# Local attention with the scores transposed at birth: keys on partitions, a fixed shift in the exponent, row sums from columns of ones

## The reference, cut to what matters

```python
WIN = 16
idx = jnp.arange(s)[:, None] + jnp.arange(-WIN, 1)[None, :]
valid = idx >= 0
k_win = k_full[:, jnp.maximum(idx, 0)]
scores = jnp.einsum('bsh,bswh->bsw', x, k_win) * h ** (-0.5)
scores = jnp.where(valid[None], scores, -jnp.inf)
attn_out = jnp.einsum('bsw,bswh->bsh', jax.nn.softmax(scores, axis=-1), k_win)
x1 = _layernorm(x + attn_out, g1, be1)
...
gate = jax.nn.sigmoid(jnp.concatenate([x1, mo], axis=-1) @ Wg.T + bg)
combined = gate * x1 + (1.0 - gate) * mo
x2 = _layernorm(x1 + combined, g2, be2)
ff = jax.nn.silu(x2 @ W1.T + b1) @ W2.T + b2
```

## Time and profile before

| what | value |
|---|---|
| median of 3 runs | 2090.1 us (2085.8, 2090.1, 2090.33) |
| the profiled execution: its own time | 2084.03 us |
| its span, first to last instruction | 2082.0 us |
| mean granted TensorE clock | 0.942 |
| PE busy | 1885.0 us (91%) |
| DVE busy | 1579.9 us (76%) |
| ACT busy | 1091.3 us (52%) |
| POOL busy | 651.0 us (31%) |

### The profile page before, as it was taken

How to read it: one execution, slowest core, us unless ns; L and a number is a source line. 1 busy time by engine, 2 the same in 40 slices (tenths; PEclk the granted TensorE clock), 3 DMA queues, 4 the chain that set the end, 5 groups by cost and what they waited for, 6 DMA issues and landing times.

```text
span 2082.0 us, 32807 instructions
## 1 busy us (share of the span) xinstructions
PE 1885.0 (91%) x11942; PEld 1683.8 (81%) x11942; DVE 1579.9 (76%) x4165; ACT 1091.3 (52%) x1890; POOL 651.0 (31%) x872
## 2 busy tenths in 40 slices
PE   5888978999999999999579995889999769999996
PEld 4677867998989998898469984779989659999995
DVE  5665637999999999999758874678988736666663
ACT  4554544556656666655456643444544235555552
POOL 3333200123333343334513322123444412322332
PEclk9999989999999999999789997989999679999998
DMA  5545331012212112110234413213322212332210
GB/s 173 175 159 189 135 108 61 21 52 70 84 60 76 55 57 86 55 64 24 88 100 133 134 56 112 72 61 103 95 64 62 75 59 65 100 100 74 67 55 19
DMA packets 132344, 176.86 MB, mean 85 GB/s; under 512 B 11470, under 2 KB 115541, under 8 KB 132056
## 3 DMA queue, kind: packets, MB, share of 16 engines
q1 hardware_dynamic: 121432, 159.74, 24.0%
q0 software_dynamic: 10752, 15.04, 2.2%
HBM read 113.19 MB, written 76.41 MB: 91 GB/s over the span
## 4 chain that ended last, share of the span: by engine, by line
PE 71%; DVE 17%; DMA 4%; issue 4%; ACT 2%; POOL 1%; SPq 1%; POOLq 0%; DVEq 0%; ACTq 0%
PE ps L362 63%; PE ps L386 5%; DVE bst L1346 3%; DMA xa<-in_x 2%; PE ps L657 2%; DVE xl L1360 1%; DVE xl L1365 1%; DVE fl L1534 1%; DVE kl L1371 1%; DVE f1l L1418 1%; DVE xl L1568 1%; POOL d_p L2131 1%; SPq L2259 1%; DVE pay L1654 1%; DVE hl L1434 0%
## 5 line engine op out<-in xcount | busy, mean ns | idle before, releaser
L362 PE MATMUL ps<-wslotA,fh 128*128 128x256 f32 x1792 | 327.5, 283 | 0.0
L362 PEld LDWEIGHTS ps<-wslotA,fh 128*128 128x128 f32 x1792 | 284.1, 191 | 6.8 <-DVE fl L1534 0.2
L1534 DVE TENSOR_TENSOR fl<-fF,fh 128x512 fp32r<-128x512 f32 x320 | 214.7, 684 | 92.7 <-ACT fF L1016 92.7
L2126 POOL TENSOR_TENSOR smalls<-smalls,powers 128x4 f32<-128x4 f32 x104 | 41.2, 396 | 714.0 <-DVE smalls L1349 713.9
L362 PE MATMUL ps<-wslotA,fl 128*128 128x256 f32 x896 | 253.4, 283 | 0.0
L362 PE MATMUL ps<-x2h,wslotA 128*128 128x512 f32 x512 | 181.4, 406 | 0.0
L362 PEld LDWEIGHTS ps<-wslotA,fl 128*128 128x128 f32 x896 | 171.3, 191 | 0.0
L1015 ACT ACTIVATE fh<-ps,b1e 128x512 fp32r<-128x512 f32 x128 | 88.3, 690 | 148.5 <-PE ps L362 146.3
L2131 POOL DMA_INDIRECT d_p<-pay,sut x128 | 137.5, 1074 | 65.1 <-issue 38.5
L362 PE MATMUL ps<-wslotB,fh 128*128 128x256 f32 x768 | 139.8, 283 | 0.0
L362 PE MATMUL ps<-eh,wslotB 128*128 128x512 f32 x384 | 126.6, 396 | 4.1 <-DVE el L1732 4.1
(11 more groups left out here) (349 smaller groups left out, 5424.4 us busy)
## 6 DMA issues: line engine op xcount, KB each, us to landing
stage<-in_w SPq DMA_DIRECT2D x16, 1024.0 KB, 5.7
d_p<-pay SPq DMA_DIRECT2D x24, 528.0 KB, 5.3
pay<-d_p SPq DMA_DIRECT2D x24, 528.0 KB, 3.8
xa<-in_x SPq DMA_DIRECT2D x16, 512.0 KB, 6.3
d_h<-hh SPq DMA_DIRECT2D x16, 512.0 KB, 4.6
d_h<-hl SPq DMA_DIRECT2D x16, 512.0 KB, 2.7
xl<-in_x SPq DMA_DIRECT2D x16, 512.0 KB, 3.9
hh<-d_h SPq DMA_DIRECT2D x16, 512.0 KB, 5.3
```

What stands on the lines that cost most here:

```text
L362: return pe.matmul(o, a, b, start=start, stop=stop, skip_group_check=True)
L1534: ve.tensor_tensor(fl[n % 2][:, half(k)], fF[n % 2][:, half(k)], f32(fh[n % 2][:, half(k)]), ALU.subtract).then_inc(S["low"], 1)
L2126: last(po.tensor_tensor(t[:, 8:12], mv_of(t)[:, :, 1], eps, ALU.add))
```

## The change

Scores are computed with keys on partitions: for each tile of 128 keys the 128 queries of the same tile and the first 16 of the next one (144 columns). What comes out of the exponent is already the stationary operand of `attend`, so `p_t`, `p_turned` and `pT` go, and with them one unit of the ring. The shift of the exponent is the constant -16, so the maximum, its bias and the four separate activations become one activation over 576 columns. Each tile of `xl` gets two more columns that hold ones (258 a tile, 4128 bytes a group), and `attend` gives the row sums in column 256. 258 columns don't fit twice into a bank, so `attend` now takes two units, AV0 and AV1, one after the other. `halo` copies one tile and only in even groups. `sc` is double. `Wg1T` and `Wg2T` are loaded into `pay[0]`, which makes them wait for the zero fills that read it, and the load of `xl3` waits for nothing of `qc`.

```diff
 def scores(g):
     evacuated("XT", g)
     ps = unit("SC", g)
...
+    for i in range(4):
+        n = 144 if i < 3 else 128
         for c in range(2):
             o = c * 512 + i * 128
-            t = mm(ps[:, i * 256:i * 256 + 160], q[:, o:o + 128], q[:, o - 32:o + 128], c == 0 and i == 2, c == 1)
+            mm(ps[:, i * 256:i * 256 + n], q[:, o:o + 128], q[:, o:o + n], c == 0 and i % 2 == 0, c == 1)
+    for c in range(2):
+        t = mm(ps[:, 896:912], before[:, c * 512 + 384:c * 512 + 512], q[:, c * 512:c * 512 + 16], False, c == 1)
     t.then_inc(S["sc"], 1)
...
-def p_t(g):
-    pe.wait_ge(S["ex"], g + 1)
-    ps = unit("PT", g)
...
 def attend(g):
-    evacuated("PT", g)
-    pe.wait_ge(S["halo"], g + 1)
-    ps = unit("AV", g)
+    pe.wait_ge(S["ex"], g + 1)
+    pe.wait_ge(S["halo"], g // 2 + 1)
+    x, p = xl[g % 4], sc[g % 2]
+    units = [unit("AV", g, k) for k in range(2)]
     for i in range(4):
+        mm(units[i // 2][:, half(i % 2, 258)], p[:, i * 144:i * 144 + 128], x[:, i * 258:i * 258 + 258],
+           True, i == 0 and g % 2 == 0)
     for i in range(0 if g % 2 else 1, 4):
+        o = (i - 1) % 4 * 144 + 128
+        rows_ = x[:, (i - 1) * 258:i * 258] if i else halo_t
+        t = mm(units[i // 2][0:16, half(i % 2, 258)], p[:, o:o + 16], rows_, False, True)
+        if i % 2:
+            t.then_inc(S["av"], 1)
...
 def exponent(g):
-    act.wait_ge(S["mx"], g + 1)
-    s = sat_at(g)
-    for i in range(4):
-        q = sc[:, i * 160:(i + 1) * 160]
-        t = act.activation(q, q, ACT.Exp, bias=s[:, 4 + i:5 + i], scale=1.0 / 16.0, accum_out=s[:, 8 + i:9 + i])
+    u, q = ring.of("SC", g), sc[g % 2][:, 0:576]
+    act.wait_ge(u.free, u.before + 1)
+    act.activation(q, q, ACT.Exp, bias=bound, scale=1.0 / 16.0).then_inc(S["ex"], 1)
...
 def memory(n):
     if n == 0:
+        ve.wait_ge(S["mpe"], 2)
+        ve.wait_ge(S["prep_dve"], 1)
+        for i in range(4):
+            ve.memset(v3(xl[i], 4, 258)[:, :, 256:258], 1.0)
...
 def halo(g):
+    if g % 2 == 0:
+        ve.wait_ge(S["xn"], g + 1)
+        if g:
+            ve.wait_ge(S["av"], 2 * g)
+        ve.tensor_copy(halo_t, xl[g % 4][:, 774:1032]).then_inc(S["halo"], 1)
...
 def masked(g):
-    last(ve.tensor_reduce(s[:, 0:4], scv, AX.X, ALU.max))
-    ve.tensor_scalar(s[:, 4:8], s[:, 0:4], -1.0 / 16.0, None, ALU.mult).then_inc(S["mx"], 1)
+    ve.tensor_tensor(v3(sc[g % 2][:, 0:576], 4, 144), v3(u.ap, 4, 256)[:, :, 0:144],
+                     bandm.unsqueeze(1).to_broadcast([128, 4, 144]), ALU.add).then_inc(u.free, 1)
...
 def attended(g):
-    u, s, x = ring.of("AV", g), sat_at(g), xv(xl[g % 4])
+    s, x = sat_at(g), xw(xl[g % 4])
+    ve.wait_ge(S["av"], 2 * g + 2)
+    for k in range(2):
+        u = ring.of("AV", g, k)
+        pv = v3(u.ap, 2, 512)
+        last(ve.reciprocal(s[:, 12 + 2 * k:14 + 2 * k], pv[:, :, 256]))
+        for i in (2 * k, 2 * k + 1):
+            t = ve.scalar_tensor_tensor(x[:, i, :], pv[:, i % 2, 0:256], s[:, 12 + i:13 + i], x[:, i, :],
+                                        ALU.mult, ALU.add)
+        t.then_inc(u.free, 1)
...
     square(mw_v, "mem_W", S["qabc"])
+if s == 12:
+    sp.wait_ge(S["fill"], 384)
     square(wg2_v, "Wg2T", S["qabc"])
     square(wg1_v, "Wg1T", S["qabc"])
```

More of the change, by code:

```diff
@@ L32 @@
 TILES_AT = SMALL_AT + 20608
[L33 removed]
+CONST_AT = TILES_AT + 19 * PAGE + 128
 class Count:
@@ L381, in mm256, with turn @@
                 return t
-            def turn(ps, x, signal):
+            def turn(ps, x, signal, stride=256):
                 for c in range(2):
@@ L581, in x_t @@
                 pe.wait_ge(S["xn"], g + 1)
-                turn(unit("XT", g), xl[g % 4], S["xnT"])
+                turn(unit("XT", g), xl[g % 4], S["xnT"], 258)
             def scores(g):
@@ L586, in scores @@
                 ps = unit("SC", g)
[L587 to L593, removed]
+                q, before = xT[g % 2], xT[(g - 1) % 2 if g % 2 else 0]
@@ L643, in x2_t @@
                 pe.wait_ge(S["x2"], g + 1)
-                turn(unit("X2T", g), xl[g % 4], S["x2T"])
+                turn(unit("X2T", g), xl[g % 4], S["x2T"], 258)
             def t_t(which, g, x):
@@ L1515, in clear_pay @@
             def clear_pay():
-                for i in (1, 2):
+                for i in range(3):
                     ve.memset(pay_v[i][:, :, 261:264], 0.0)
@@ L1557, in masked @@
-                s = sat_at(g)
-                ve.wait_ge(u.free, u.before + 1)
-                last(ve.tensor_reduce(s[:, 0:4], scv, AX.X, ALU.max))
-                ve.tensor_scalar(s[:, 4:8], s[:, 0:4], -1.0 / 16.0, None, ALU.mult).then_inc(S["mx"], 1)
-            def attended(g):
-                u, s, x = ring.of("AV", g), sat_at(g), xv(xl[g % 4])
-                ve.wait_ge(S["ex"], g + 1)
-                last(ve.reciprocal(s[:, 12:16], s[:, 8:12]))
-                ve.wait_ge(S["av"], g + 1)
-                for i in range(4):
-                    t = ve.scalar_tensor_tensor(x[:, i, :], u.ap[:, i * 256:(i + 1) * 256], s[:, 12 + i:13 + i], x[:, i, :],
-                                                ALU.mult, ALU.add)
-                t.then_inc(u.free, 1)
+                if g >= 2:
+                    ve.wait_ge(S["av"], 2 * (g - 1))
@@ L1572, in stats_1st @@
             def stats_1st(g):
-                u = ring.of("AV", g)
-                stats(xv(xl[g % 4]), mv_of(sm(0, g)), S["var1"], [(u.free, u.before + 1)] * 4)
+                u = [ring.of("AV", g, k) for k in range(2)]
+                stats(xw(xl[g % 4]), mv_of(sm(0, g)), S["var1"], [(u[i // 2].free, u[i // 2].before + 1) for i in range(4)])
             def affine_1st(g):
-                affine(xv(xl[g % 4]), sm(0, g), g1_r, be1_r, (S["rs1"], g + 1))[3].then_inc(S["x1"], 1)
+                affine(xw(xl[g % 4]), sm(0, g), g1_r, be1_r, (S["rs1"], g + 1))[3].then_inc(S["x1"], 1)
```

106 lines of the change are left out of this document (36 added, 70 removed), and 2 rows, old and new, of the table S.

## The result

The changed kernel has a median of 2104.24 us (2099.52 to 2112.98, six runs) beside 2090.22 us before: ratio 1.0074, 95% interval 1.0051 to 1.0097. It is slower by 14.0 us, where 16.3 were forecast, though TensorE, VectorE and ScalarE all have less work. The profiled execution took 2101.55 us, its span 2099.8.

The account below looks back on a forecast made before the run. In the group stage TensorE and VectorE are both nearly full and TensorE sets the pace. Terms +12.0, -3.0, -2.0, -0.6 and +9.9 for the clock give +16.3 on 2087.6: 2104 us, 8-in-10 range 2087 to 2116.

Parts of the forecast that it names:

- The wait: From step 3, W13 waits until AV0 is emptied, T0 (gates' end) + 11.86 us; 2.0 to 2.5 idle; net +12.0.
- What TensorE saves: Each group-stage step loses p_t, 0.79 us, and 0.20 of the scores; about 1.0 us shorter with nothing else.
- Steps 0 to 2: First group-stage steps, where prefix takes no unit and W13 doesn't wait: they only gain, 3 x 0.99 = -3.0 us.
- Step -1: Before step 0, TensorE no longer waits for the copy of pT: -2.0 us.
- The end of step 13: TensorE's 0.62 us wait for VectorE there goes, since VectorE is now early: -0.6 us.
- The clock: The new wait halves TensorE's clock in half of 11 steps, at 1.8 us each: +9.9, bounds 0 and +20.
- four likenesses: Four earlier TensorE idle stretches of 2.55 to 3.15 us, two followed by half clock; basis for the factor of half.
- The sum: Whole kernel: +6.4 us without clock and +9.9 for the clock make +16.3, giving 2104 us.
- The load of `xl3`: Issued some 3 us sooner beside W2's load; bounds 0 and +1.3 us, taken as 0.
- The clock holds: Rival: the wait at W13 comes but the clock doesn't fall; +6.4 us, 2094; chance 0.2.
- falls in every step: Rival: the clock falls in each of the 11 steps; +26 us, 2114; chance 0.12.
- Faster: Rival: AV0 emptied early enough, T0 + 9.8 for full gain, steps longer from T0 + 10.8; -17 us, 2071; chance 0.12.

Follow-up runs that it names:

- before_two_units: Kernel before with one edit, attend in two units instead of one; 2117.71 us, ratio to before 1.0147.
- sums_after_w13: Changed kernel with the prefix sums on TensorE moved from ahead of W13 to behind it; 2084.43 us, ratio to before 0.9995.
- early_release: Changed kernel with VectorE emptying attend's units ahead of two subtractions for W12's group; 2086.56 us, ratio to before 0.9991.
- late release: Changed kernel with attend's second unit emptied first, so AV0 is emptied one microsecond later; 2125.85 us, ratio to before 1.0175.
- best_old_drain: Changed kernel with prefix sums behind W2, their emptying and the sent tokens' statistics later on VectorE, only where attend has a group left; 2070.89 us, ratio to before 0.9916.
- sums_after_w2: Changed kernel with the prefix sums behind the W2 that follows W13, and VectorE's emptying of them behind the second LayerNorm's affine; ratio to before 0.9997.
- warm_fill: Changed kernel with eight never-read matmuls of 512 columns a step between the prefix sums and W13; ratio to before 1.0050.
- sums_before_w12: Changed kernel with the prefix sums ahead of W12 and VectorE's emptying of them ahead of its subtractions; 2137.23 us, ratio to before 1.0240.

## Why the prediction was right

**The wait.** Right in place and size. T0 to W13 is 11.87 us (forecast 11.86), idle 2.03 and 2.47 (2.0 to 2.5), the step 44.86 (44.76). Eleven of these steps, wait less saving and no clock in it, cost 12.35 x 1.1 = 13.6 us (12.0). The excess lies behind W13: from there to the next T0 it is 32.99 us and not 32.90 (the scores take 2.28 us, 0.14 less and not 0.20), and 0.3 is step 9's. That the turn of the ring makes the wait, and not the new operands, is shown by before_two_units; that it goes to whoever takes AV0's unit, by sums_after_w13; that it is paid one for one, by early and late release.

**What TensorE saves.** 0.99 us a step was forecast. best_old_drain, which waits for 0.2 us in ten steps, has 42.74 where the kernel before has 43.66: 0.92. Steps 0 to 2 came out 3.15 us shorter (forecast 3.0). Step -1, from the first gates to T0 of step 0, went from 43.77 to 41.85 us, -1.9 (-2.0).

**The end of step 13.** This step of the sum failed: -0.6 was forecast, because VectorE "is now early". The gap is as long as in the earlier trace rows:

```profile
957.27 0.44 PE L390 MATMUL ps<-ident,xl 128*128 128x128 f32 x2 [0.61 <-DVE xl L1347]
```

The reason given for the term was wrong. This gap is the end of a chain that starts at TensorE itself: x2's transposes X2T, ScalarE's copy `x2h`, VectorE's `x2l`, logits and affine, then X1T. From X2T to X1T it takes 7.31 us in step 13 of before and of the change, and 7.31 to 7.33 in all other traces but sums_after_w2 (8.15), whether W13 waits for 3 us, 0.8 or not at all. VectorE's lead can't shorten it; VectorE spends it standing, as in this step of the change:

```profile
946.45 0.69 DVE L1520 TENSOR_TENSOR fl<-fF,fh 128x512 fp32r<-128x512 f32 x1 [2.12 <-ACT fF L1011]
...
951.32 1.29 DVE L1353 TENSOR_TENSOR x2l<-ps,x2h 128x512 fp32r<-128x512 f32 x2 [0.41 <-ACT x2h L878]
```

The first is for W13's result, which reaches VectorE by way of ScalarE, the second inside the chain. VectorE's waits in the ten middle steps (us in total, times, longest):

```profile
DVE gt L1563 <- PE ps L366: 20.3, 19, 1.3
DVE fl L1520 <- ACT fF L1011: 10.6, 10, 2.2
DVE x2l L1353 <- ACT x2h L878: 4.4, 10, 0.7
```

That is 3.5 us a step; the forecast had some 3, all at the gates.

**The clock.** Right in kind, too high in both factors: 11 x 0.5 x 1.8 = 9.9 was forecast, four falls of 1.5 us came, 6.4 by the fill. The 1.8 came from `attend` alone at half clock; a fall in these steps costs 1.5. The "half" came from four likenesses, and nothing in the prediction derives it. That four is near 5.5 has luck in it: the same four steps fell in both traces of the change, and the shorter waits of before_two_units gave five.

**The sum.** +16.3 was forecast. The stage, which holds all terms but the loads, grew by 14.6 and 14.8 us in two traces, and the medians by 14.0 and 17.8. Terms: +13.6 wait, -3.15, -1.9, 0, +6.4 = +14.9. The forecast's errors partly cancel: the wait was put 1.6 too low and the end 0.6, the clock 3.5 too high. That the median met 2104 to 0.3 us is luck, since the same two kernels differed by 14.0 and by 17.8 us. The load of `xl3`, put at 0 with a bound of +1.3, can't be told from the start's own spread.

**The rivals.** "The clock holds" and "falls in every step" are both realised, by warm_fill and sums_before_w12, and neither by the change. "Faster" priced its condition well as far as it was tried: it let a step grow from W13 at T0 + 10.8 on, and with W13 at 10.66 (early_release) the steps have the 43.66 us of before. A release by T0 + 9.8 was never run. Letting W13 meet another unit wasn't enough by itself (sums_after_w13).

## What to carry to other kernels

When a piece of work takes one more buffer of a round-robin pool, redo the pairing of every later user with the one n turns back, and ask which engine empties that one and when; here a sum of 8-column products decided it. An order written by hand is balanced for its old durations: after a saving, look for the next wait, where an engine first runs without pause up to a hand-over and then stands. And make such moves only in the steady part of the loop, since in its last steps other work is on the path.

## What the runs showed of the hardware

The granted clock fell behind waits much shorter than those of the earlier trace rows. Without a fall in eleven steps: waits of 0.82 and 1.26 us at W13, and of 0.97 and 1.40 at the sums. With falls: 1.11 and 1.55 us (five), 2.03 and 2.47 (four), 3.01 and 3.45 (ten), 3.8 us at `attend` (eleven). In the change each fall began 0.8 to 1.3 us after W13 had started. A fall goes to 1.2 GHz, from 2.4, and costs 1.5 us of the step here. Length alone doesn't order them, since the shorter waits of before_two_units gave one fall more than those of the change; why is open. The Trainium skill's "TensorE: Matmul & The Clock Gate", section "Why this matters for your kernels", warns of idle gaps above about 3 us; the nine falls behind shorter ones in these two kernels disagree.

Products nobody reads, 1.84 us of them a step in the middle of the wait, took all four falls away and made the stage 6.4 us shorter (warm_fill): here TensorE lost more by waiting than the wait.
